# Window attention of a vision block: the row maxima in seven groups of 8 by 8 queries instead of eight of 8 by 7

## The chip, the cores and the metric

The kernel runs on one core of a Trainium2 chip. Its time is the device time of one execution, in microseconds (us). Below, PE is TensorE (PEld its weight loads), DVE is VectorE, ACT is ScalarE, POOL is GpSimd and SP is SyncE, which here only issues DMAs. ACTq and SPq are the DMA issues of ACT and SP.

## The reference

Two images of 128 channels and 56 by 56 pixels go through three attentions that are mixed by a gate, a gated MLP and a LayerNorm. The change touches only the third attention: every pixel looks at the 7 by 7 pixels around it (edge padded), in 8 heads of 16 channels.

```python
DIM, HEADS, BS, TOPK, WIN = (128, 8, 8, 4, 7)
padded = jnp.pad(feat, ((0, 0), (pad, pad), (pad, pad), (0, 0)), mode='edge')
patches = jnp.stack([padded[:, dy:dy + Hx, dx:dx + Wx, :] for dy in range(WIN) for dx in range(WIN)], axis=3)
...
q = _lin(Q, wq_w[2], wq_b[2]).reshape(Bx, Nq, h, d)
k = _lin(patches, wk_w[2], wk_b[2]).reshape(Bx, Nq, WIN * WIN, h, d)
v = _lin(patches, wv_w[2], wv_b[2]).reshape(Bx, Nq, WIN * WIN, h, d)
attn = jax.nn.softmax(jnp.einsum('bnhd,bnwhd->bnhw', q, k) * scale, axis=-1)
y_win = jnp.einsum('bnhw,bnwhd->bnhd', attn, v).reshape(Bx, Nq, C)
```

## The kernel before

The program has three stages: projections with the two block attentions (to about 331 us), the window attention (to about 560 us), and the MLP. Only the window attention changes.

**Jobs and steps.** The window attention has 14 jobs: two images by seven bands of 8 pixel rows. A band is 56 columns by 8 rows, 448 queries, and its keys are 62 columns by 14 rows. A job is 14 steps: the keys come in 7 blocks of 9 columns, each done for 4 heads at a time. All engines run one loop over steps `q` (`STEP_RANGE`), and the place in a job is `r = q % 14`. In every step PE does the scores of step q (L881: 4 matmuls, keys by queries, 120, 72 or 64 queries wide), ACT the exponential of them (L1083), and PE the products with the values for step q - 3 (L897). Scores alternate between two PSUM banks, so scores of step q wait for the exponential of step q - 2.

**The maxima.** Softmax needs a number to subtract from each query's scores before the exponential. It rides in the score matmul: row 126 and 127 of `Q` hold minus the maximum as two bf16 parts. It is made 12 steps (`LEAD`) before the job's first step. One group of maxima, here called A0 to A7, is `maxima` on PE (L840): 8 matmuls, one a head, of 64 queries by 182 keys, into a slot of two PSUM banks. A subgroup is 7 columns of 8 rows, 56 queries; the matmul takes 64 columns of queries and the last 8 repeat. DVE reduces a slot over the keys (L1456). Every two groups DVE splits the result into two bf16 parts (L1462, L1464), PE transposes it (L867, here called S0 to S3), DVE copies the transpose to `nT` (L1469), and SP sends `nT` by DMA into rows 126 and 127 of `Q` (L450). Scores of the steps in `TILE_NEEDED` wait for that DMA.

**Slots.** Groups A, transposes S, and two jobs at a band's end share two slots in turn: D (L908, `spread` times `RB`, the reciprocal sums brought to all channels; DVE multiplies by them, L1474) and Y (L914, the output projection; DVE adds it to `XT`, L1484). Use n of the slots waits until DVE has read use n - 2 (`slot_free`). Where each stands is a list of steps:

```python
MAX_AT = (0, 1, 3, 5, 7, 8, 10, 12)
BEHIND = 1
TURN_AT = (4, 8, 11, 15)
TILE_NEEDED = {0: 0, 2: 1, 6: 2, 8: 3}
SUMS_AT, RECIP_AT, PARTS_AT, NORM_AT, Y_AT = 17, 21, 22, 27, 30
```

With the lead of 12, `MAX_AT` 0 stands at r = 2, and so on: before, A0 to A7 stand at r = 2, 3, 5, 7, 9, 10, 12, 0 and S0 to S3 at r = 6, 10, 13, 3. The group `BEHIND` is done after the step's products, not ahead of its scores. D stands at r = 13 behind the products, Y at r = 2 behind the products.

**The chain to D.** At r = 3 SP moves the sums of the job that just ended to `SR` (L464). At r = 7 DVE takes the reciprocal (L1446), ahead of everything else that it has in that step. POOL multiplies by the gate and splits into three bf16 parts (L587 to L597, which counts `w_parts`). At r = 8 SP sends them to `RB` in three DMAs (L471). D waits for them.

**SP's list.** SP issues DMAs in the order of its program and waits where a wait stands. For step q it takes in turn: the `nT` transfer of a transpose that stands in step q - 1 (it waits for DVE's copy), a load of values `Vw` in even steps (L459), the sums, and the three transfers to `RB`. ACT issues the loads of a later band's keys and queries (L384, L386) in its own stream, behind the exponentials of r = 13, 3 and 7; the largest part goes at r = 13.

Of the kernel before, what the change touches and what calls it, by code (L numbers as in the profile page):

```python
# [36 lines left out]
KCOLS = SUBC + WIN - 1  # L37
# [7 lines left out]
MQ = 64  # L45
# [7 lines left out]
QSPAN = HEADS * BAND + MQ - SUB  # L53
# [72 lines left out]
def build(nc, x, wts, vecs, rows, pjb, dwr, c32, cmask, out):  # L126
    ctx = ExitStack()
    with ctx:
# [108 lines left out]
        with ExitStack() as s3:  # L237
            K = [KQ0[:, 0:KSPAN]] + [sb(f"K{n}", [128, KSPAN], BF16, s3)[:] for n in (1, 2)]
            QB = [KQ0[:, KSPAN:KSPAN + QSPAN]] + [sb(f"Q{n}", [128, QSPAN], BF16, s3)[:] for n in (1, 2)]
            Q = [q[:, 0:HEADS * BAND].rearrange("p (h n) -> p h n", h=HEADS) for q in QB]  # L240
            Vw = [sb(f"Vw{n}", [KEYS, VROW], F32, s3) for n in range(VRING)]
            P = [sb(f"P{n}", [KEYS, 4 * max(BQ)], F32, s3) for n in range(4)]
            wn = [sb(f"wn{n}", [128, 2, PAIRS], F32, s3) for n in range(2)]
            wnb = [sb(f"wnb{n}", [128, 2, 2, PAIRS], BF16, s3) for n in range(2)]
            nT = [sb(f"nT{n}", [HEADS, 2, TILE], BF16, s3) for n in range(2)]
# [76 lines left out]
        SUBN = SUBS * JOBS  # L322
# [5 lines left out]
        MAX_AT = (0, 1, 3, 5, 7, 8, 10, 12)  # L328
        BEHIND = 1
        TURN_AT = (4, 8, 11, 15)  # L330
        TILE_NEEDED = {0: 0, 2: 1, 6: 2, 8: 3}
# [10 lines left out]
        def turned_at(q):  # L342
            found = []
            for k, at0 in enumerate(TURN_AT):
                j = job_at(q + LEAD, at0)
                if j is not None:
                    found.append(TILES * j + k)
            return found

        pa, pa_order = {}, {}  # L350
        for q in STEP_RANGE:
            jobs, behind = [], []
            for k, at0 in enumerate(MAX_AT):
                if job_at(q + LEAD, at0) is not None:
                    (behind if k == BEHIND else jobs).append(("A", SUBS * job_at(q + LEAD, at0) + k))
# [10 lines left out]
        assert sum(k == "A" for k, n in pa_order) == SUBN  # L366
# [22 lines left out]
        def _(sp):  # L389
# [51 lines left out]
            for q in STEP_RANGE:  # L441
# [4 lines left out]
                for n in turned_at(q - 1):  # L446
                    j, c = divmod(n, TILES)
# [38 lines left out]
        def _(pool):  # L486
# [132 lines left out]
        def _(pe):  # L619
# [204 lines left out]
            pe.wait_ge(sem("w_pad"), 2 * BUFS)  # L824
# [7 lines left out]
            def maxima(n, slot, order):  # L832
                j, c = divmod(n, SUBS)
# [3 lines left out]
                for h in range(HEADS):  # L837
                    p, e = divmod(h, 2)
                    first = h * KBAND + SUBC * c * KROWS
                    last = mm(PS[MQ * e:MQ * (e + 1), 2 * slot + p // 2, p % 2 * SKEYS:(p % 2 + 1) * SKEYS],  # L840
                              QB[j % BUFS][0:SHIFT0, h * BAND + c * SUB:h * BAND + c * SUB + MQ], K[j % BUFS][0:SHIFT0, first:first + SKEYS], start=True, stop=True)
# [12 lines left out]
            for q in STEP_RANGE:  # L854
# [4 lines left out]
                for kind, n, slot, order in pa.get(q, ()):  # L859
                    if kind == "A" and n % SUBS != BEHIND:  # L860
                        maxima(n, slot, order)
                    if kind == "S":
# [3 lines left out]
                        for c in range(2):  # L866
# [309 lines left out]
        def _(dve):  # L1176
# [261 lines left out]
            for q in STEP_RANGE:  # L1438
# [9 lines left out]
                for kind, n, slot, order in pa.get(q, ()):  # L1448
                    dve.wait_ge(sem("w_slot"), order + 1)
                    if kind == "A":  # L1450
                        tl, c = divmod(n, 2)
# [5 lines left out]
                        if c == 1:  # L1457
# [7 lines left out]
                    if kind == "S":  # L1465
                        if n >= 2:
                            dve.wait_ge(sem(f"w_shift{n % 2}"), 16 * (n // 2))
                        src = PS[0:HEADS, 2 * slot, 0:128].bitcast(BF16).rearrange("p (s e n) -> p e s n", s=2, e=2)[:, :, :, 0:SUB]
                        ve.tensor_copy(nT[n % 2][:].rearrange("p e (s n) -> p e s n", s=2), src).then_inc(sem("w_slot_read"), 1)  # L1469
# [144 lines left out]
```

## Time and profile before

| what | value |
|---|---|
| median of 3 runs | 770.14 us (766.46 to 771.43) |
| the profiled execution, its own time | 772.19 us |
| span of its trace | 770.4 us |
| busy: PE, DVE, ACT, POOL | 689.2, 607.4, 351.2, 214.8 us |
| mean granted TensorE clock | 0.962 |

The span is what the trace covers, and the profiled execution's own time is 1.8 us more. Busy time says how long an engine had an instruction in it, not what it waited for. The 14139 instructions of the trace are read below by stretches of the window attention, since what a change in one stage is worth is decided there.

### The profile page before, as it was taken

How to read it: one execution, taken by the hardware profiler on the slowest of the kernel's cores; microseconds unless marked ns; L12 is line 12 of the kernel's file. 1: busy time of each engine (PE TensorE's matmuls, PEld its weight loads, DVE VectorE, ACT ScalarE, POOL GpSimd, SP SyncE). 2: the span in 40 equal slices, each digit the busy share in tenths (PEclk: the TensorE clock that was granted, in tenths of full speed). 3: DMA queues.
4: the chain of work that ended last, by engine and by line, in shares of the span. 5: the costliest groups of instructions: out<-in, count | busy, mean ns of one | idle time of the engine just before them, and what ended most of it. 6: DMA issues, size and time to landing. Idle time of an engine off the chain costs nothing.

```text
span 770.4 us, 14139 instructions
## 1 busy us (share of the span) xinstructions
PE 689.2 (89%) x5055; PEld 365.3 (47%) x5055; DVE 607.4 (79%) x1236; ACT 351.2 (46%) x618; POOL 214.8 (28%) x331
## 2 busy tenths in 40 slices
PE   4998987789788989878999999999889999999996
PEld 2543443445344444444555555555434545455553
DVE  6996657878788799867777777777369879999873
ACT  2175423444444344305555555555534062646676
POOL 2026112545445454507100110010190436400000
PEclk9999988979999899969999999999999999999998
DMA  6004221533233339724656656762000000000101
GB/s 245 0 0 109 54 54 45 132 80 79 71 81 93 81 95 252 176 72 131 158 154 180 180 156 167 181 171 47 18 2 0 1 0 0 1 21 22 42 22 63
DMA packets 52663, 66.22 MB, mean 86 GB/s; under 512 B 10606, under 2 KB 48498, under 8 KB 50738
## 3 DMA queue, kind: packets, MB, share of 16 engines
q1 hardware_dynamic: 49426, 43.08, 21.3%
q10 hardware_dynamic: 3168, 22.24, 10.5%
q8 instruction: 41, 0.67, 0.4%
q14 instruction: 28, 0.23, 0.1%
HBM read 43.03 MB, written 21.57 MB: 84 GB/s over the span
## 4 chain that ended last, share of the span: by engine, by line
PE 50%; DVE 22%; issue 8%; ACT 6%; DMA 2%; POOL 1%; SPq 0%; ACTq 0%; DVEq 0%; POOLq 0%
PE banks L959 12%; PE banks L897 7%; PE banks L881 6%; PE banks L840 5%; DVE AC L1204 4%; DVE mx L1392 4%; PE banks L914 3%; DVE sm L1407 2%; DVE X L1484 2%; PE banks L852 2%; DVE SEB L1395 1%; PE banks L710 1%; ACT pf L1022 1%; ACT PTB L1067 1%; PE banks L782 1%
## 5 line engine op out<-in xcount | busy, mean ns | idle before, releaser
L1083 ACT ACTIVATE P<-banks 126x480 f32<-126x480 f32 (+2 forms) x196 | 101.1, 521 | 112.1 <-PE banks L881 98.6
L959 PE MATMUL banks<-FP,PTB 128*128 128x392 f32 x384 | 129.8, 493 | 2.1 <-DVE c L1487 1.2
L1456 DVE TENSOR_REDUCE wn<-banks 128x4 f32<-128x728 f32 x112 | 102.1, 913 | 26.0 <-PE banks L840 24.2
L1204 DVE SCALAR_TENSOR_TENSOR AC<-XT,vec,AC 128x1540 f32<-128x1540 f32 (+5 forms) x48 | 118.0, 2462 | 1.1
L959 PEld LDWEIGHTS banks<-FP,PTB 128*128 128x128 f32 x384 | 72.7, 190 | 56.9 <-DVE FP L1524 2.2
L549 POOL TENSOR_TENSOR SEB<-SEB,rg 112x392 f32<-112x392 f32 x112 | 61.2, 567 | 111.2 <-DVE rg L1414 111.2
L1058 ACT ACTIVATE SEB<-SEB 112x424 f32<-112x424 f32 x56 | 31.2, 558 | 113.1 <-DVE SEB L1395 113.1
L897 PE MATMUL banks<-P,Vw 126*17 126x120 f32 (+2 forms) x1568 | 73.3, 260 | 0.0
L519 POOL TENSOR_TENSOR pk<-pr,pk 128x434 bf16<-128x434 f32 (+1 forms) x42 | 47.7, 1136 | 45.4 <-DVE pk L1307 45.4
L804 PE MATMUL banks<-PTB,VP 106*128 106x448 f32 x112 | 54.0, 570 | 6.2 <-issue 3.7
L782 PE MATMUL banks<-Af,XT 128*112 128x424 f32 x112 | 54.2, 568 | 0.0
L587 POOL TENSOR_TENSOR SR<-SR,SRG 64x56 f32<-64x56 f32 x14 | 4.2, 297 | 171.6 <-DVE SR L1446 171.6
L1302 DVE TENSOR_TENSOR pr<-pf,pk 128x434 f32<-128x434 f32 (+1 forms) x42 | 27.6, 658 | 27.1 <-ACT pk L1023 27.0
L881 PE MATMUL banks<-Q,K 128*128 128x120 bf16 (+2 forms) x504 | 45.2, 213 | 2.0 <-DMA Q<-nT 1.7
L1392 DVE TENSOR_REDUCE mx<-banks 112x8 f32<-112x392 f32 x112 | 36.8, 370 | 10.3 <-PE banks L783 10.3
L840 PE MATMUL banks<-K,Q 126*64 126x182 bf16 x576 | 37.0, 251 | 3.3 <-DVE c L1486 3.0
L1395 DVE TENSOR_TENSOR SEB<-banks,mx 112x392 f32<-112x392 f32 x112 | 37.2, 374 | 1.9
L791 PE MATMUL banks<-cst,SEB 112*106 112x112 f32 x224 | 34.5, 278 | 4.3 <-POOL SEB L549 4.2
L1204 DVE SCALAR_TENSOR_TENSOR FP<-X,vec,FP 128x3025 f32<-128x3025 f32 (+5 forms) x16 | 36.2, 2263 | 0.6
L643 PE MATMUL banks<-X,diag 128*128 128x440 f32 (+3 forms) x90 | 35.0, 552 | 1.3 <-DMA X<-in_x 1.3
L1407 DVE TENSOR_REDUCE sm<-SEB 112x8 f32<-112x392 f32 x112 | 36.1, 364 | 0.0
L881 PEld LDWEIGHTS banks<-Q,K 128*128 128x128 bf16 x504 | 26.1, 98 | 20.7 <-issue 6.0
(247 smaller groups left out, 1195.6 us busy)
## 6 DMA issues: line engine op xcount, KB each, us to landing
k_parts<-pk SPq DMA_DIRECT2D x84, 108.5 KB, 3.4
Vw<-v_rows SPq DMA_DIRECT2D x84, 66.9 KB
q_parts<-pk SPq DMA_DIRECT2D x42, 112.0 KB, 2.3
K<-k_parts ACTq DMA_DIRECT2D x7, 651.0 KB, 5.8
v_rows<-vst SPq DMA_DIRECT2D x14, 263.5 KB
X<-in_x SPq DMA_DIRECT2D x2, 1568.0 KB, 8.3
K<-k_parts ACTq DMA_DIRECT2D x7, 434.0 KB, 3.7
out_y<-zs SPq DMA_DIRECT2D x7, 392.0 KB, 2.4
```

Of the source, the lines that this page charges most:

```text
L549: g.tensor_tensor(dst, src, by, ALU.mult).then_inc(sem("c_norm"), 1)
L782: mm(s, XT[:, img, ds(t * BAND + c * TILE, TILE)], Af[img][:], start=True, stop=False)
L804: last = mm(bank(4 + img, C, BAND), VP[img][:, j, :], PT[img][:, j, :], start=(j == 0), stop=(j == PAIRS - 1))
L840: last = mm(PS[MQ * e:MQ * (e + 1), 2 * slot + p // 2, p % 2 * SKEYS:(p % 2 + 1) * SKEYS], QB[j % BUFS][0:SHIFT0, h * BAND + c * SUB:h * B ...
L881: last = mm(PS[:, 4 + q % 2, g * BQ[b]:(g + 1) * BQ[b]], K[j % BUFS][:, first:first + 128], Q[j % BUFS][:, h, BLOCK * BX0[b]:BLOCK * BX0[b ...
L897: last = mm(PS[QUAD * g:QUAD * g + VH, 6 + u, BLOCK * BX0[b]:BLOCK * BX0[b] + BQ[b]], Vw[s % VRING][0:BKEYS[b], VH * h:VH * (h + 1)], P[p ...
L959: last = mm(bank(2 + place_in_unit, C, ZPIX), WT[:, dy, part, C * grp:C * (grp + 1)], D[:, part, QROWS * q + dy:QROWS * (q + 1) + dy, :].r ...
L1083: a(P[q % 4][0:BKEYS[b], 0:4 * BQ[b]], PS[0:BKEYS[b], 4 + q % 2, 0:4 * BQ[b]], ACT.Exp).then_inc(sem("w_exp"), 1)
L1204: return ve.scalar_tensor_tensor(out=o, in0=src(ro + dy, rn, co + dx, cn), scalar=v(wcol + t), in1=o, op0=ALU.mult, op1=ALU.add)
L1392: ve.tensor_reduce(mx[:, ty, :, :], groups(ps, ty), AX.X, ALU.max).then_inc(sem("c_max"), 1)
L1407: ve.tensor_reduce(sm[:, ty, :, :], groups(Ex[r % 2], ty), AX.X, ALU.add).then_inc(sem("c_sum"), 1)
L1456: ve.tensor_reduce(dst, src, AX.X, ALU.max, negate=True).then_inc(sem("w_slot_read"), 1)
```

## The change

A group of maxima takes 8 by 8 queries, 64 of 64 useful, and 14 by 14 = 196 keys instead of 13 by 14 = 182. A job then has seven groups, A0 to A6. Tiles of two groups are 128 queries wide instead of 112, and the fourth tile of a job holds one group: one transpose, and a `nT` transfer half as wide. The padding of `Q` and its three memsets go. The places in the steps change with it: A0 to A6 stand at r = 2, 4, 6, 7, 9, 10, 0 and S0 to S3 at r = 7, 10, 13, 3. The fourth tile is needed at r = 10 instead of 8. Everything else keeps its place.

```diff
-KCOLS = SUBC + WIN - 1
+MCOLS = 8
+MGROUPS = SIDE // MCOLS
+MTILES = -(-MGROUPS // 2)
+KCOLS = MCOLS + WIN - 1
...
-MQ = 64
+MQ = BLOCK * MCOLS
...
-        MAX_AT = (0, 1, 3, 5, 7, 8, 10, 12)
+        MAX_AT = (0, 2, 4, 5, 7, 8, 12)
         BEHIND = 1
-        TURN_AT = (4, 8, 11, 15)
-        TILE_NEEDED = {0: 0, 2: 1, 6: 2, 8: 3}
+        TURN_AT = (5, 8, 11, 15)
+        TILE_NEEDED = {0: 0, 2: 1, 6: 2, 10: 3}
...
+        def tile_groups(k):
+            return min(2, MGROUPS - 2 * k)
...
-                    dst = Q[j % BUFS][SHIFT0:SHIFT0 + 2, :, c * TILE:(c + 1) * TILE]
-                    sp.dma_start(dst, nT[n % 2][:]).then_inc(sem(f"w_shift{n % 2}"), 16)
+                    cols = tile_groups(c) * MQ
+                    dst = Q[j % BUFS][SHIFT0:SHIFT0 + 2, :, 2 * MQ * c:2 * MQ * c + cols]
+                    sp.dma_start(dst, nT[n % 2][:, :, 0:cols]).then_inc(sem(f"w_shift{n % 2}"), 16)
...
-                        for c in range(2):
+                        for c in range(tile_groups(n % MTILES)):
...
-                        if c == 1:
+                        if c == tile_groups(k // 2) - 1:
```

On PE, from the step r = 4 of a job (before: from the end of r = 3) to r = 7, with A groups as L840 before and L846 now, the transpose as L867 and L873, scores L881 and L887, products L897 and L903. Before:

```order
L840 MATMUL banks<-FP 64x182 x8
L881 MATMUL banks<-Q,K 128x120 x4
L897 MATMUL banks<-P,Vw 17x72 x4
L840 MATMUL banks<-FP 64x182 x8
L881 MATMUL banks<-Q,K 128x120 x4
L897 MATMUL banks<-P,Vw 17x120 x4
L867 MATMUL banks<-identb,wnb 8x128 x2
L881 MATMUL banks<-Q,K 128x120 x4
L897 MATMUL banks<-P,Vw 17x120 x4
L840 MATMUL banks<-FP 64x182 x8
```

Now:

```order
L887 MATMUL banks<-Q,K 128x120 x4
L903 MATMUL banks<-P,Vw 17x72 x4
L846 MATMUL banks<-FP 64x196 x8
L887 MATMUL banks<-Q,K 128x120 x4
L903 MATMUL banks<-P,Vw 17x120 x4
L846 MATMUL banks<-FP 64x196 x8
L887 MATMUL banks<-Q,K 128x120 x4
L903 MATMUL banks<-P,Vw 17x120 x4
L846 MATMUL banks<-FP 64x196 x8
L873 MATMUL banks<-identb,wnb 8x128 x2
```

A1 has moved behind the products of r = 4, A2 to the head of r = 6, and the transpose S0, which stood alone at the head of r = 6, now stands in r = 7 right behind A3.

On DVE, in the same place of the program, from the reduction of A1 on (reductions L1456 and L1463, split L1462/L1464 and L1469/L1471, copy to `nT` L1469 and L1477, reciprocal L1446 and L1452). Before:

```order
L1456 TENSOR_REDUCE wn0<-banks 128x4 [waits w_slot]
L1462 CAST wnb0<-wn0 128x2x4 [waits w_slot,w_slot_read]
L1464 TENSOR_TENSOR wnb0<-wn0,wnb0 128x2x4 [waits w_high]
L1456 TENSOR_REDUCE wn1<-banks 128x4 [waits w_split,w_slot]
L1469 COPY nT0<-banks 8x224 [waits w_shift0,w_slot]
L1446 RECIPROCAL SR0<-SR0 64x56 [waits w_recips0,w_sums0]
L1456 TENSOR_REDUCE wn1<-banks 128x4 [waits w_slot]
L1462 CAST wnb1<-wn1 128x2x4 [waits w_slot,w_slot_read]
L1464 TENSOR_TENSOR wnb1<-wn1,wnb1 128x2x4 [waits w_high]
```

Now:

```order
L1463 TENSOR_REDUCE wn0<-banks 128x4 [waits w_slot]
L1469 CAST wnb0<-wn0 128x2x4 [waits w_slot,w_slot_read]
L1471 TENSOR_TENSOR wnb0<-wn0,wnb0 128x2x4 [waits w_high]
L1463 TENSOR_REDUCE wn1<-banks 128x4 [waits w_split,w_slot]
L1452 RECIPROCAL SR0<-SR0 64x56 [waits w_recips0,w_sums0]
L1463 TENSOR_REDUCE wn1<-banks 128x4 [waits w_slot]
L1469 CAST wnb1<-wn1 128x2x4 [waits w_slot,w_slot_read]
L1471 TENSOR_TENSOR wnb1<-wn1,wnb1 128x2x4 [waits w_high]
L1477 COPY nT0<-banks 8x256 [waits w_shift0,w_slot]
```

The copy of S0 to `nT0` stood ahead of the reciprocal and now stands behind it and behind the reduction and the split of A3.

On SP, from r = 7 to r = 11 (`nT` transfers L450 and L457, values L459 and L466, `RB` L471 and L478). Before:

```order
L450 DMA Q1<-nT0 2x8x112 [waits w_slot_read]
L459 DMA Vw6<-v_rows 126x1x136 [waits w_products]
L471 DMA RB0<-SB0 4x16x56 [waits rb_zero,w_parts]
L471 DMA RB0<-SB0 4x16x56 x2
L459 DMA Vw7<-v_rows 126x1x136 [waits w_products]
L450 DMA Q1<-nT1 2x8x112 [waits w_slot_read]
```

Now:

```order
L457 DMA Q1<-nT0 2x8x128 [waits w_slot_read]
L466 DMA Vw6<-v_rows 126x1x136 [waits w_products]
L478 DMA RB0<-SB0 4x16x56 [waits rb_zero,w_parts]
L478 DMA RB0<-SB0 4x16x56 x2
L466 DMA Vw7<-v_rows 126x1x136 [waits w_products]
L457 DMA Q1<-nT1 2x8x128 [waits w_slot_read]
```

Only the width of the `nT` rows differs: the transfer of S0 stands ahead of the three to `RB` and the transfer of S1 behind them, before and now.

## Rows read from the trace of the kernel before

**Rows 1.** Stretch 405 to 420 us: busy time by engine, granted clock, DMA share, GB/s
```profile
405.00:420.00 15.00, 14.54 (x246) 8.29 (x238) 11.66 (x25) 8.00 (x16) 1.41 (x6) 1.00 0.62 168
```

**Rows 2.** PE's timeline in one job: start, us, line, op, [idle before <- releaser]
```profile
443.32 0.51 PE L840 MATMUL banks<-K,Q 126*64 126x182 bf16 x8
443.76 0.38 PE L881 MATMUL banks<-FP 128*128 128x120 bf16 x4
...
444.40 0.51 PE L840 MATMUL banks<-K,Q 126*64 126x182 bf16 x8
...
445.13 0.38 PE L881 MATMUL banks<-FP 128*128 128x120 bf16 x4
...
448.06 0.55 PE L908 MATMUL banks<-RB,spread 128*128 128x448 bf16 x2
...
450.45 0.38 PE L881 MATMUL banks<-Q,K 128*128 128x120 bf16 x4
...
453.98 0.50 PE L840 MATMUL banks<-K,Q 126*64 126x182 bf16 x8 [0.44 <-DVE c L1486]
...
454.98 0.50 PE L840 MATMUL banks<-K,Q 126*64 126x182 bf16 x8
```

**Rows 3.** DVE's timeline in the same job
```profile
441.38 0.25 DVE L1469 COPY nT<-banks 8x224 bf16<-8x224 bf16 x1
441.56 0.48 DVE L1446 RECIPROCAL SR<-SR 64x56 f32<-64x56 f32 x1
...
444.95 0.92 DVE L1456 TENSOR_REDUCE wn<-banks 128x4 f32<-128x728 f32 x1 [0.16 <-PE banks L840]
...
446.19 0.26 DVE L1469 COPY nT<-banks 8x224 bf16<-8x224 bf16 x1
...
454.53 0.92 DVE L1456 TENSOR_REDUCE wn<-banks 128x4 f32<-128x728 f32 x1 [0.34 <-PE banks L840]
...
455.77 0.91 DVE L1456 TENSOR_REDUCE wn<-banks 128x4 f32<-128x728 f32 x1
...
456.78 0.48 DVE L1446 RECIPROCAL SR<-SR 64x56 f32<-64x56 f32 x1
```

**Rows 4.** SP's own DMA issues in the same job
```profile
441.66 0.71 SPq L450 DMA_DIRECT2D Q<-nT  x1
442.42 0.78 SPq L459 DMA_DIRECT2D Vw<-v_rows  x1
443.91 2.37 SPq L471 DMA_DIRECT2D RB<-SB  x3
446.32 0.83 SPq L459 DMA_DIRECT2D Vw<-v_rows  x1
447.20 0.70 SPq L450 DMA_DIRECT2D Q<-nT  x1
```

**Rows 5.** ACT's issue of a band's largest load, same job
```profile
447.84 0.56 ACTq L384 DMA_DIRECT2D FP<-k_parts  x1
```

**Rows 6.** DVE groups by shape, 100 to 330 us
```profile
L1392 DVE TENSOR_REDUCE mx<-banks 112x8 f32<-112x392 f32 x56 | 31.4, 560 | 10.3 <-PE banks L783 10.3
```

**Rows 7.** DMA issues from 376 to 528 us: KB each, median us to landing
```profile
K<-k_parts ACTq DMA_DIRECT2D x6, 651.0 KB, 5.8
...
Q<-q_parts ACTq DMA_DIRECT2D x6, 336.0 KB, 6.7
```

**Rows 8.** The second job: S3's transfer issued, and the scores that wait for it
```profile
361.14 0.69 SPq L450 DMA_DIRECT2D Q<-nT  x1
...
366.32 0.38 PE L881 MATMUL banks<-Q,K 128*128 128x120 bf16 x4 [1.42 <-DMA Q<-nT]
```

**Rows 9.** The stage's end: the transfers to RB and the D behind them
```profile
547.66 1.84 SPq L471 DMA_DIRECT2D RB<-SB  x3
...
550.96 0.55 PE L908 MATMUL banks<-RB,spread 128*128 128x448 bf16 x2
```

**Rows 10.** The stage's start: the last group ahead of the first scores
```profile
341.50 0.82 PE L840 MATMUL banks<-FP 126*64 126x182 bf16 x8 [0.70 <-DVE wn L1456]
```

More of the change, by code:

```diff
@@ L52 @@
 KSPAN = HEADS * KBAND + 64
-QSPAN = HEADS * BAND + MQ - SUB
+QSPAN = HEADS * BAND
 QUAD = 32
@@ L244, in build @@
             wnb = [sb(f"wnb{n}", [128, 2, 2, PAIRS], BF16, s3) for n in range(2)]
-            nT = [sb(f"nT{n}", [HEADS, 2, TILE], BF16, s3) for n in range(2)]
+            nT = [sb(f"nT{n}", [HEADS, 2, 2 * MQ], BF16, s3) for n in range(2)]
             OB = [sb(f"OB{n}", [128, 2, BAND], F32, s3) for n in range(2)]
@@ L321, in build @@
         STEPS = STEPJ * JOBS
-        SUBN = SUBS * JOBS
+        GROUPS_ALL = MGROUPS * JOBS
         LEAD = 12
@@ L346, in turned_at @@
                 if j is not None:
[L347 removed]
+                    found.append(MTILES * j + k)
             return found
@@ L354, in build @@
                 if job_at(q + LEAD, at0) is not None:
-                    (behind if k == BEHIND else jobs).append(("A", SUBS * job_at(q + LEAD, at0) + k))
+                    (behind if k == BEHIND else jobs).append(("A", MGROUPS * job_at(q + LEAD, at0) + k))
             jobs += [("S", n) for n in turned_at(q)]
@@ L365, in build @@
                 pa.setdefault(q, []).append((kind, n, order % 2, order))
-        assert sum(k == "A" for k, n in pa_order) == SUBN
+        assert sum(k == "A" for k, n in pa_order) == GROUPS_ALL
+        def tile_groups(k):
+            return min(2, MGROUPS - 2 * k)
         NQ = IMAGES * QUARTERS
@@ L832, in maxima @@
             def maxima(n, slot, order):
-                j, c = divmod(n, SUBS)
+                j, c = divmod(n, MGROUPS)
                 if c == 0:
@@ L838, in maxima @@
                     p, e = divmod(h, 2)
-                    first = h * KBAND + SUBC * c * KROWS
+                    first = h * KBAND + MCOLS * c * KROWS
                     last = mm(PS[MQ * e:MQ * (e + 1), 2 * slot + p // 2, p % 2 * SKEYS:(p % 2 + 1) * SKEYS],
-                              QB[j % BUFS][0:SHIFT0, h * BAND + c * SUB:h * BAND + c * SUB + MQ], K[j % BUFS][0:SHIFT0, first:first + SKEYS], start=True, stop=True)
+                              QB[j % BUFS][0:SHIFT0, h * BAND + c * MQ:h * BAND + (c + 1) * MQ], K[j % BUFS][0:SHIFT0, first:first + SKEYS], start=True, stop=True)
                 last.then_inc(sem("w_slot"), 1)
@@ L859, in _ @@
                 for kind, n, slot, order in pa.get(q, ()):
-                    if kind == "A" and n % SUBS != BEHIND:
+                    if kind == "A" and n % MGROUPS != BEHIND:
                         maxima(n, slot, order)
@@ L901, in _ @@
                 for kind, n, slot, order in pa.get(q, ()):
-                    if kind == "A" and n % SUBS == BEHIND:
+                    if kind == "A" and n % MGROUPS == BEHIND:
                         maxima(n, slot, order)
@@ L1450, in _ @@
                     if kind == "A":
-                        tl, c = divmod(n, 2)
+                        j, k = divmod(n, MGROUPS)
+                        tl, c = MTILES * j + k // 2, k % 2
                         if c == 0 and tl >= 2:
@@ L1467, in _ @@
                             dve.wait_ge(sem(f"w_shift{n % 2}"), 16 * (n // 2))
-                        src = PS[0:HEADS, 2 * slot, 0:128].bitcast(BF16).rearrange("p (s e n) -> p e s n", s=2, e=2)[:, :, :, 0:SUB]
-                        ve.tensor_copy(nT[n % 2][:].rearrange("p e (s n) -> p e s n", s=2), src).then_inc(sem("w_slot_read"), 1)
+                        parts = tile_groups(n % MTILES)
+                        src = PS[0:HEADS, 2 * slot, 0:MQ * parts].bitcast(BF16).rearrange("p (s e n) -> p e s n", s=parts, e=2)
+                        ve.tensor_copy(nT[n % 2][:, :, 0:MQ * parts].rearrange("p e (s n) -> p e s n", s=parts), src).then_inc(sem("w_slot_read"), 1)
                     if kind == "D":
```

7 lines of the change are left out of this document (3 added, 4 removed).

## The prediction

> **What bounds the kernel now.** I read the stretches of the window attention first. In the full pace of that stage PE is busy 14.54 of 15.00 us at full granted clock and DVE 11.66 [rows 1]. So PE's own row of work sets the pace, and DVE has room of a fifth. Then I read PE's timeline over one job: a group of maxima holds PE for 0.44 us (443.32 to 443.76), and scores and products of a step for 0.64 us (443.76 to 444.40) [rows 2]. The one wait of any size in a job is 0.44 us ahead of A1, for DVE's reading of Y. A job takes 15.22 us, from one reciprocal to the next (441.56 to 456.78) [rows 3]. Last I read what is nearly late, because a planned order moves work against deadlines that no busy share shows: D waits for three DMAs that start with the reciprocal, and each tile's maxima must have landed in `Q` before its scores. I measure all from R, the start of the reciprocal. Before, SP issues the transfer of S0 at R + 0.10, the values, then RB at R + 2.35, S1's transfer at R + 5.64 [rows 4]; ACT issues the largest band load at R + 6.28 [rows 5]; D runs at R + 6.50 [rows 2].
>
> **Sizes of the pieces now.** A group is 14 keys wider of 182, so at most 0.44 x 14/182 = 0.034 us longer: 0.47. A reduction of 392 elements takes 0.560 us and one of 728 takes 0.92 [rows 3, 6], 1.07 ns an element, so 784 elements take 0.98. DVE does seven of 0.98 instead of eight of 0.92, 0.5 us less a job; it is not the bound, so that alone is worth nothing. The lone transpose of the fourth tile saves about 0.1: a pair with its short wait fills 445.13 - 444.40 - 0.44 = 0.29 [rows 2]. The padding memsets are on POOL ahead of the stage and worth 0.
>
> **PE's row of work, D to the next R.** Before, D to A1 is 453.98 - 448.06 = 5.92 [rows 2]. Now two groups in it are wider (+0.06), S3 is half (-0.10), the wait for Y goes (-0.44), since A1 stands one step later, and that step's scores and products come ahead of A1 (454.98 - 453.98 - 0.44 = 0.56). That makes 6.00, and A1 ends at 6.47. But A2 now stands only one step before the reciprocal, so DVE decides R: 0.11 from A1's end to its reduction, 1.24 + 0.06 to A2's (454.53 to 455.77), 0.89 for A2's reduction until the next instruction starts (1.01 to the reciprocal less 0.18 for the copy between, + 0.06) [rows 2, 3]. R comes at 6.47 + 0.11 + 1.30 + 0.89 = 8.77 after D; before it was 8.72.
>
> **PE's row of work, R to D.** Before 6.50. A3 now lies ahead of R (-0.44), r = 12 has no group (-0.44), A4 and A5 are wider (+0.06). S0 shares a slot with A2, so it waits until A2 is reduced, at R + 0.09, and about 0.1 for the release, and takes 0.2 (+0.40). PE is ready for it 0.64 + 0.47 + 0.64 + 0.47 = 2.22 after A1's end, DVE at 2.5: a new wait of 0.3. S1, with a longer reduction ahead, +0.06. D could run at R + 6.14. By PE alone a job would be 8.77 + 6.14 = 14.91, a gain of 0.3. This is what the change could bring.
>
> **The first cost: SP's list.** SP's order is the same before and now, and there lies the trouble. S0's transfer stands ahead of RB and waits for DVE's copy. Before, the copy ended at R + 0.07. Now it is behind the reciprocal (0.42, with the 0.06 to 0.08 that neighbouring DVE instructions overlap), and from a reduction that closes a tile to the end of its copy it is 446.19 + 0.26 - 444.95 = 1.50, + 0.06 [rows 3]: R + 1.98. Then 0.76 for S0's issue and 0.82 for the values [rows 4]: RB starts at R + 3.58 instead of R + 2.35, though POOL has the parts ready as early as before. Three issues take 1.84 [rows 9] to 2.37 [rows 4]; I take 2.2: R + 5.78. Landing is bounded from above by the stage's end, where D ran 1.46 after the last issue's end (550.96 - 549.50) [rows 9], from below by 0. I take 1.4, since a DMA of any kind here needs more than 3 us from its issue to its landing [rows 7]. D runs at R + 7.25, so a job takes 16.0: +0.8. With the lower end D is not late at all, and with the upper it is +1.0.
>
> **The second cost: what stands behind RB.** The values and then S1's transfer follow at R + 5.82 and R + 6.70. ACT's largest load does not wait for D; it goes 0.22 before D's place in PE's row (448.06 - 447.84) [rows 2, 5]: R + 5.92. Before, S1's transfer went 0.64 ahead of this load; now it goes 0.8 behind it. What that costs the trace shows once: S3's transfer in the second job, issued at 361.14 among band loads, held its scores until 366.32, 5.2 us [rows 8]. The load itself needs 5.8 us, and its queries, issued 0.6 later, 6.7 [rows 7]. So S1's maxima land between R + 11.7 and R + 13.2; I take the middle, 12.5. If the transfer slipped through as before, where it was there within 450.45 - 447.20 = 3.25 [rows 2, 4], it would land by R + 9.95. The scores of r = 2 need it 450.45 - 448.06 + 0.06 = 2.45 after D, at R + 9.7. They wait 2.8 us, and R follows 8.77 - 2.45 = 6.32 later. A job takes 12.5 + 6.32 = 18.8 us, +3.6 (from +2.8 to +4.3). While that wait is last, D's exact time costs nothing.
>
> The Trainium skill ("DMA: Bandwidth & Descriptors", section "Queues, rings and completion order") says that each DMA engine takes turns between the rings of SP and ACT, a packet at a time. By that rule a small transfer need not wait for a whole band load; the 5.2 us speak against it here. By the rule the time would be that of the first rival.
>
> **The sum.** There are 14 jobs. S0, RB and S1 of three neighbouring jobs meet in 12 job times, and in 10 of them the largest load goes too (it stops three bands before the end). 10 x 3.6 + 2 x 0.8 = 37.6. Gains: ahead of the first scores there is one group less, 0.82 + 0.70 = 1.5 [rows 10]; the wait of 1.42 [rows 8] goes, since the fourth tile is needed two steps later, and the first job has PE's gain of 0.3: together 3. So +34.6 on the profiled execution's 772.2, 806.8. The median shown is 2.05 lower: **804.8 us**, 4.5% slower.
>
> **Rivals.** (1) S1's transfer passes the band load, and only D is late: 12 x 0.8 - 3 = +6.6, **777 us**. For it: transfers issued just ahead of a load pass. Against: the 5.2 us. (2) RB's last transfer is caught too: it is issued about 0.7 ahead of the load, as S1's was before, and that one passed; this margin is thin. Then D runs at R + 5.92 + 5.8 + 0.1 = 11.8, a job takes 20.6 (+5.4, up to +6.9): 54 + 1.6 - 3 = +52.6, **823 us**, up to 838. (3) The other side: SP does not hold RB back, as S0's copy is done early enough. RB, S0 and S1 then run as before and PE's gain stays: 13 x 0.3 + 3 = -7, **763 us**, faster. It decides at a copy that ends by R + 0.75 (RB at R + 2.35); I have 1.98, and DVE's order puts 1.5 us of work between, so it needs the copy to be there at less than half of that. (4) The stage's PE falls to a lower granted clock in the new waits. Rows of before have full clock at 14.54 busy of 15; with waits of 4 us in 19 nothing here shows a fall, and I price it only in the upper end.
>
> **Chances.** My forecast 60%, (1) 15%, (2) 12%, (3) 9%, the rest 4%. The range takes in (1) at its lower part and most of (2): 775 to 830. A measurement of this kernel tells 1%, about 7.7 us, from no change. Faster by more than that needs (3) to do better than I price it: 5%. Within it lie most of (3) and half of (1): 14%. Slower: 81%.
>
> **What would show it.** In the profile of the changed kernel: the reduction at 0.98 us; reciprocals 18.8 us apart (16.0 in the last two jobs); RB's issues 3.6 us behind the reciprocal; a wait of about 1.1 us of D for the DMA to RB and one of about 2.8 of the scores at r = 2 for the DMA from `nT`; no wait of A1 for Y. I am wrong if S1's transfer is issued ahead of the large load, if the `nT` wait is under 1 us, or if S0's copy comes within 1 us of the reciprocal.

## The result and the profile after

The changed kernel takes 816.31 us (median of 4 runs, 815.39 to 820.88), the kernel before 769.21 beside it (4 runs, 766.46 to 771.43). The ratio is 1.063, with a 95% interval from 1.057 to 1.068: slower, by more than the 4.5% forecast and inside the range. The profiled execution took 815.39 us, its span is 813.2, the mean granted clock 0.950.

The whole page says little. PE was busy 689.2 us and is now busy 697.1. These are the page's busy times, and two of its groups with the waits ahead of them, and the chain that ended last by line:

```profile
PE 697.1 (86%) x4929; PEld 364.7 (45%) x4929; DVE 602.2 (74%) x1222; ACT 349.4 (43%) x618; POOL 215.7 (27%) x328
...
PE banks L965 13%; DMA Q<-nT 5%; PE banks L887 5%; PE banks L903 4%; PE banks L920 4%; DVE mx L1398 4%; DVE wn L1463 3%; DMA FP<-nT 3%; PE banks L846 2%; DVE AC L1210 2%; DVE sm L1413 2%; PE banks L858 1%; DVE SEB L1401 1%; ACT pf L1028 1%; ACT PTB L1073 1%
...
L1463 DVE TENSOR_REDUCE wn<-banks 128x4 f32<-128x784 f32 x98 | 94.2, 965 | 21.7 <-PE banks L846 20.2
...
L887 PE MATMUL banks<-Q,K 128*128 128x120 bf16 (+2 forms) x504 | 47.3, 220 | 18.7 <-DMA Q<-nT 17.9
```

The reduction takes 0.965 us (0.98 forecast). Two transfers from `nT`, into `Q` and into `FP` (the same kind of buffer, the bands use both in turn), hold 8% of the chain. PE's waits in the window attention say how often (us in total, times, longest):

```profile
PE banks L887 <- DMA Q<-nT: 17.9, 7, 3.4
PE banks L914 <- DMA RB<-SB: 10.1, 12, 1.3
PE banks L887 <- DMA FP<-nT: 6.8, 3, 3.0
```

Scores wait for the maxima of S1 in ten jobs, 24.7 us in all. D waits in twelve jobs, 10.1 in all. Both counts are those of the forecast. The kernel before had 1.7 us of waits for `nT` in two waits, and none of D.

**One job, from its reciprocal at R = 461.04.** First DVE's timeline (start, us, line, operation): the copy of S0 comes behind the reciprocal and A3's reduction, as in the order.

```profile
461.04 0.48 DVE L1452 RECIPROCAL SR<-SR 64x56 f32<-64x56 f32 x1
461.44 0.90 DVE L1463 TENSOR_REDUCE wn<-banks 128x4 f32<-128x784 f32 x1
...
462.69 0.27 DVE L1477 COPY nT<-banks 8x256 bf16<-8x256 bf16 x1
```

Then SP's own issues, and ACT's of the largest load. They answer to [rows 4, 5]:

```profile
462.99 0.71 SPq L457 DMA_DIRECT2D Q<-nT  x1
463.75 0.78 SPq L466 DMA_DIRECT2D Vw<-v_rows  x1
464.62 1.93 SPq L478 DMA_DIRECT2D RB<-SB  x3
466.60 0.83 SPq L466 DMA_DIRECT2D Vw<-v_rows  x1
467.48 0.70 SPq L457 DMA_DIRECT2D Q<-nT  x1
```

```profile
466.93 0.56 ACTq L390 DMA_DIRECT2D FP<-k_parts  x1
```

RB is issued at R + 3.58 (2.35 before). S1's transfer goes at R + 6.44 and the load at R + 5.89: the transfer was 0.64 ahead of the load and is now 0.55 behind it. PE's timeline shows the two waits, and the projection Y (L920) behind the second:

```profile
467.98 0.55 PE L914 MATMUL banks<-RB,spread 128*128 128x448 bf16 x2 [0.76 <-DMA RB<-SB]
...
473.11 0.58 PE L887 MATMUL banks<-Q,K 128*128 128x120 bf16 x4 [2.63 <-DMA Q<-nT]
...
473.97 3.36 PE L920 MATMUL banks<-ON,W 128*128 128x448 f32 x4
```

D runs at R + 6.94, the scores at R + 12.07. The next reciprocal comes at 481.78, so this job takes 20.74 us. Y takes 3.36, and it takes 1.77 in the kernel before. The same four matmuls of scores take 0.58, and 0.38 before [rows 2].

**What S1's transfer waits for.** The trace also holds a record of every DMA packet. ACT's load is 48 packets of 13,888 bytes. In this job they start between 468.65 and 470.93, and the last has ended by 471.86. S1's transfer is 16 packets of 256 bytes, of about 0.03 us each. They start at 471.70 to 471.98, which is 4.2 us behind the issue at 467.48 and 1.1 us ahead of the scores. From 468.86 to 471.69 only ACT's queue (q10; SP's is q1) has packets: those of the load, and the first of the queries' load behind it (packets, MB, share of 16 engines):

```profile
q10 hardware_dynamic: 63, 0.59, 77.7%
```

In the kernel before, S1's transfer was issued at 447.20. Its 16 packets (224 bytes) start at 448.56 to 448.68, and the first of the load at 449.19. So the transfer itself is short in both. Behind the load it doesn't start before nearly all of the load has been moved.

**All jobs.** Windows cut from one reciprocal to the next, four of the ten with an S1 wait (length, busy of PE, PEld, DVE, ACT, POOL, then the granted clock, DMA share, GB/s):

```profile
424.18:442.23 18.05, 14.66 (x237) 8.18 (x237) 11.37 (x27) 7.94 (x16) 1.43 (x6) 1.00 0.53 144
442.23:461.04 18.81, 16.07 (x237) 8.59 (x237) 11.35 (x27) 8.05 (x16) 1.43 (x6) 0.91 0.51 140
461.04:481.78 20.74, 17.05 (x237) 9.05 (x237) 11.34 (x26) 8.02 (x16) 1.43 (x6) 0.84 0.47 124
481.78:499.89 18.11, 13.85 (x221) 7.75 (x221) 11.38 (x27) 7.33 (x15) 1.43 (x6) 1.00 0.53 134
```

Only two of the ten have the full clock. They take 18.05 and 18.11 us; the other eight take 18.81 to 20.84 with clocks of 0.84 to 0.92. The ten take 196.34 us (363.47 to 559.81) where the kernel before took 152.63 (365.06 to 517.69): +43.7. The last jobs add 0.8. The stage begins with the first group of maxima. These are its lines, first before, then now:

```profile
332.14 0.89 PE L840 MATMUL banks<-FP 126*64 126x182 bf16 x16 [1.92 <-DVE banks L1435]
327.73 0.87 PE L846 MATMUL banks<-FP 126*64 126x196 bf16 x16 [1.92 <-DVE banks L1441]
```

From there to the first reciprocal it takes 32.92 us before and 35.75 now: +2.8. From the first group to the last reciprocal that is 223.46 and 270.78 us: +47.3, as much as the medians differ (47.1). So the window attention holds all of the difference. The two spans differ by only 813.2 - 770.4 = 42.8, because in this execution the stages ahead, which the change leaves as they are but for three memsets, ended 4.4 us earlier. In the fourteen traces of this record the first group starts anywhere from 324.72 to 332.14. In the two jobs of full clock S1's maxima are the limit and nothing else is late. In the rest a second cost comes on top, which I had given no chance of its own: a lower clock.

### The profile page after: what moved, and what is told of

The parts are those of the page before. It is cut to its first block, busy times and chain, and to the rows that moved or that the text cites. A ratio compares the mean times of both kernels' runs of the same rounds, so it can differ in the third digit from the quotient of the medians.

```text
span 813.2 us, 13870 instructions
## 1 busy us (share of the span) xinstructions
PE 697.1 (86%) x4929; PEld 364.7 (45%) x4929; DVE 602.2 (74%) x1222; ACT 349.4 (43%) x618; POOL 215.7 (27%) x328
## 4 chain that ended last, share of the span: by engine, by line
PE 42%; DVE 22%; DMA 9%; issue 8%; ACT 6%; SPq 1%; POOL 1%; ACTq 1%; DVEq 0%; POOLq 0%
PE banks L965 13%; DMA Q<-nT 5%; PE banks L887 5%; PE banks L903 4%; PE banks L920 4%; DVE mx L1398 4%; DVE wn L1463 3%; DMA FP<-nT 3%; PE banks L846 2%; DVE AC L1210 2%; DVE sm L1413 2%; PE banks L858 1%; DVE SEB L1401 1%; ACT pf L1028 1%; ACT PTB L1073 1%
## 5 line engine op out<-in xcount | busy, mean ns | idle before, releaser
L1463 DVE TENSOR_REDUCE wn<-banks 128x4 f32<-128x784 f32 x98 | 94.2, 965 | 21.7 <-PE banks L846 20.2
L903 PE MATMUL banks<-P,Vw 126*17 126x120 f32 (+2 forms) x1568 | 75.0, 266 | 0.0
L887 PE MATMUL banks<-Q,K 128*128 128x120 bf16 (+2 forms) x504 | 47.3, 220 | 18.7 <-DMA Q<-nT 17.9
L788 PE MATMUL banks<-Af,XT 128*112 128x424 f32 x112 | 52.1, 548 | 0.0
L1492 DVE TENSOR_TENSOR X<-banks,XT 128x448 f32<-128x448 f32 x14 | 14.0, 999 | 48.3 <-PE banks L920 48.3
L887 PEld LDWEIGHTS banks<-Q,K 128*128 128x128 bf16 x504 | 27.4, 101 | 39.1 <-DMA Q<-nT 19.4
L1482 DVE TENSOR_TENSOR ON<-OB,banks 128x896 f32<-128x896 f32 x14 | 15.2, 1087 | 33.3 <-PE banks L914 33.3
```

The source lines that it names most:

```text
L788: mm(s, XT[:, img, ds(t * BAND + c * TILE, TILE)], Af[img][:], start=True, stop=False)
L887: last = mm(PS[:, 4 + q % 2, g * BQ[b]:(g + 1) * BQ[b]], K[j % BUFS][:, first:first + 128], Q[j % BUFS][:, h, BLOCK * BX0[b]:BLOCK * BX0[b ...
L903: last = mm(PS[QUAD * g:QUAD * g + VH, 6 + u, BLOCK * BX0[b]:BLOCK * BX0[b] + BQ[b]], Vw[s % VRING][0:BKEYS[b], VH * h:VH * (h + 1)], P[p ...
L1463: ve.tensor_reduce(dst, src, AX.X, ALU.max, negate=True).then_inc(sem("w_slot_read"), 1)
```

## The experiments

**1. The groups without the places.** The new geometry, with A0 to A6 and S0 to S3 in the steps that they had before. From the changed kernel:

```diff
-        MAX_AT = (0, 2, 4, 5, 7, 8, 12)
+        MAX_AT = (0, 1, 3, 5, 7, 8, 12)
-        TURN_AT = (5, 8, 11, 15)
+        TURN_AT = (4, 8, 11, 15)
```

> Seven groups of 8 by 8 at the places of before (MAX_AT 0, 1, 3, 5, 7, 8, 12 and TURN_AT 4, 8, 11, 15), so that S0 is copied ahead of the reciprocal again. My theory (the time is lost to two late transfers, which come from the place of S0): about 763 us, 760 to 767, RB issued 2.35 us behind the reciprocal, no wait of the scores for nT over 1 us. Rival (the wider groups themselves, with reductions of 0.97 us, cost the time by waits of PE for DVE): over 790 us.

Measured: 773.43 us (9 runs) beside 768.6, ratio 1.004 (0.9999 to 1.008). The loss is gone, but 760 to 767 was expected, and the gain isn't there; experiments 11 and 12 show why. Nearly all jobs are 14.99 us apart (before 15.22), but one takes 21.25. In it SP's three issues to `RB` took 2.85 us instead of 2.2:

```profile
472.21 2.85 SPq L478 DMA_DIRECT2D RB<-SB  x3
...
475.98 0.71 SPq L457 DMA_DIRECT2D FP<-nT  x1
```

```profile
482.76 0.58 PE L887 MATMUL banks<-FP 128*128 128x120 bf16 x4 [3.78 <-DMA FP<-nT]
...
483.62 3.36 PE L920 MATMUL banks<-ON,W 128*128 128x448 f32 x4
```

In a usual job S1's transfer goes 0.40 us ahead of the load (445.35 and 445.75); here 0.65 us more of SP's time put it 0.16 behind, and 6 us were lost. The faster jobs have used up part of a margin that was 0.64 to 1.12 us in the ten jobs of the kernel before.

**2. The places without the groups.** The kernel before, with eight groups of 8 by 7, in the new steps:

```diff
-        MAX_AT = (0, 1, 3, 5, 7, 8, 10, 12)
+        MAX_AT = (0, 2, 4, 5, 7, 8, 10, 12)
-        TURN_AT = (4, 8, 11, 15)
+        TURN_AT = (5, 8, 11, 15)
```

> The kernel before, eight groups of 8 by 7, with only the places moved: A1, A2 and S0 one step later, the rest as before. My theory: most of the loss is here too, 790 to 820 us. S1's transfer is then issued only 0.1 to 0.4 us behind the largest load, since A6 still stands at r = 12, so some jobs may escape the long wait. Rival (wider groups cost): 770 us, no change.

Measured: 817.56 us (4 runs), ratio 1.064 (1.058 to 1.071), the time of the changed kernel. PE's waits are the same ones:

```profile
PE banks L881 <- DMA Q<-nT: 18.0, 7, 3.3
PE banks L881 <- DMA FP<-nT: 7.5, 3, 2.7
PE banks L908 <- DMA RB<-SB: 4.9, 12, 0.5
```

So the places alone make the whole loss. D mostly runs at about R + 6.95 in both. It waits half as long here (4.9 against 10.1) because PE comes to it later, and the time is the same. S1's transfer is issued 0.11 to 0.20 us behind the load in all ten jobs, and all ten wait; none escapes.

**3. The largest load one step later.** The changed kernel, with S1's transfer ahead of the load again and D still late:

```diff
-                for part, off in enumerate((0, 4, 8)):
+                for part, off in enumerate((1, 4, 8)):
```

> The changed kernel with the largest band load one step later in ACT's stream (r = 0 of the next job instead of r = 13), so that it is issued more than 1 us behind S1's transfer. My theory: the waits of about 2.6 us of the scores at r = 2 go, D stays 0.8 us late, 767 to 776 us. Rival (the wait comes from SP's late issue alone, whatever ACT loads): no gain, about 815 us.

Measured: 785.52 us (4 runs), ratio 1.021 (1.014 to 1.027). The wait for `nT` falls from 24.7 us to 1.8 and D's stays (11.6 in 12). Moving one load takes back two thirds of the loss, so the collision of this load with this transfer is the main cause. I missed by some 10 us. The jobs are 16.2 apart, as forecast for a late D alone, but only in part for that reason: D at R + 6.98 is 0.5 later than in the kernel before. The rest goes with a new wait. The reciprocal waits for the sums' DMA, which now stands behind the moved load, 5.4 us in seven waits (0.5 in one before this edit):

```profile
DVE SR L1452 <- DMA SR<-OB: 5.4, 7, 1.8
```

The first reciprocal came at 368.47 instead of 363.47, but the stage itself began 3.4 of these 5.0 us later.

**4. RB ahead of S0's transfer in SP's list.** The changed kernel, with SP's block for `RB` moved ahead of the `nT` transfers of its step, so that D is in time:

```diff
+                j = job_at(q, PARTS_AT)
+                if j is not None:
+                    sp.wait_ge(sem("w_parts"), j + 1)
...
                 for n in turned_at(q - 1):
```

> The changed kernel with the three RB transfers ahead of S0's transfer in SP's list, nothing else. My theory: D is no longer late, but S1's transfer is still issued about 1 us behind the largest load, and that wait is the last, so the time hardly falls: 808 to 820 us. Rival (D's lateness is what costs): D's wait of 10.1 us in all comes back, 800 to 806 us or less.

Measured: 836.44 us (4 runs), ratio 1.089 (1.081 to 1.096). Worse than the change itself, and above both ranges. D no longer waits, but S0's transfer stands behind RB, and S1's behind both: at R = 432.00 S1's is issued at 439.00 with the load at 437.89, so it is 1.1 us behind the load and not 0.55. The scores wait until R + 13.2:

```profile
438.11 0.55 PE L914 MATMUL banks<-RB,spread 128*128 128x448 bf16 x2
...
445.18 0.58 PE L887 MATMUL banks<-Q,K 128*128 128x120 bf16 x4 [4.39 <-DMA Q<-nT]
...
446.04 3.35 PE L920 MATMUL banks<-ON,W 128*128 128x448 f32 x4
```

The ten jobs take 21.50 us on average (366.86 to 581.84). In this job the packets of S1's transfer start at 444.13, behind those of the load and also behind those of the queries' load, of which the last starts at 443.81. D runs 0.8 us earlier than in the changed kernel, and no job is shorter for it. Mending the first lateness lengthens the second, and the second sets the loop.

**5. Both.** RB first, and the load one step later, the edits of experiments 3 and 4 together:

> The changed kernel with both edits together: RB ahead of S0's transfer on SP, and the largest band load one step later on ACT. My theory: both waits go, jobs of 15.0 to 15.5 us, 765 to 775 us. Rival (the places themselves cost, by S0 behind A3 and the reciprocal behind two reductions): 780 us or more.

Measured: 776.89 us (4 runs), ratio 1.010 (1.001 to 1.019). Most jobs take 15.25 to 16.2 us, and the wait for `nT` is 6.3 us in 19 small ones of at most 0.9. With both waits undone the changed kernel comes within 1% of the one before. That is 2 us above my range and below the rival's. What is left of the loss stands beside two more waits: DVE's copies to `nT` wait 17.9 us in 12 for the transfers out of it, which now go behind RB, and the reciprocal 4.1 us in 8 for the sums. What the places cost without these was not separated.

**6. The old places and the later load.** Experiment 1 with the edit of experiment 3:

> The new groups at the old places, with the largest band load one step later, so that S1's transfer has over 1 us of lead on it instead of 0.4. My theory: the occasional long job of the new groups at the old places (21.2 us once in its trace, against 15.0) goes, and the time is 761 to 768 us. Rival (the long job has another cause, or the load now delays the sums): 770 us or more.

Measured: 770.39 us (10 runs), ratio 1.002 (0.999 to 1.005). Jobs are mostly 15.0 apart, none is long, and the time is still that of the kernel before. So the long job was this collision, but the time lies in the rival's range: the gain isn't there.

**7. S1's transfer late, in the kernel before.** This was to move the transfer behind the load with nothing else changed:

```diff
-        TURN_AT = (4, 8, 11, 15)
+        TURN_AT = (4, 10, 11, 15)
```

> The kernel before with only the transpose S1 two steps later (TURN_AT 4, 10, 11, 15), so that its transfer is issued behind the largest band load while RB and D keep their times. My theory (a small transfer issued behind the load waits for it): waits of 3 to 4 us of the scores at r = 2 in 10 or 11 jobs, 805 to 825 us. Rival (the collision needs SP's delayed list): 768 to 775 us.

Measured: 778.29 us (10 runs), ratio 1.013 (1.010 to 1.016). It wasn't the test that I meant. PE waited 0.35 us a job at the transpose for DVE (`wn`), so ACT's load came later too: in one job the transfer was issued at 449.28 and the load at 449.77, and in all ten it was still 0.25 to 0.49 ahead. No S1 wait came; the one `nT` wait, of 2.1 us, is at another tile. So it doesn't test the collision; it shows only that a lead of 0.25 us is enough. Experiment 9 is the test.

**8. Work for PE in the wait.** The changed kernel with 30 extra matmuls ahead of the wait for S1's maxima, in the ten jobs. Their result is overwritten and used by nothing; they only keep PE busy.

```diff
+                    if q >= 2:
+                        pe.wait_ge(sem("w_exp"), q - 1)
+                    if r == 2 and 2 <= j <= 11:
+                        for _ in range(30):
+                            mm(PS[:, 4 + q % 2, 0:128], identb[:], identb[:], start=True, stop=True)
                     if r in TILE_NEEDED:
                         n = MTILES * j + TILE_NEEDED[r]
                         pe.wait_ge(sem(f"w_shift{n % 2}"), (n // 2 + 1) * 16)
-                    if q >= 2:
-                        pe.wait_ge(sem("w_exp"), q - 1)
```

> The changed kernel with 30 extra matmuls of 128 columns (about 2.4 us of work that nothing uses, overwritten by the next scores) in jobs 2 to 11, placed where PE waits for S1's maxima at r = 2. If a part of the loss is the granted clock that falls in this wait and makes the work behind it slow (Y took 3.36 us instead of 1.77), the clock stays at 1.00 and the time falls to 803 to 810 us although PE does more. Rival (the clock is no part of it): 816 us or more.

Measured: 802.9 us (4 runs), ratio 1.043 (1.035 to 1.052). That is 13.4 us less than the changed kernel, with more work on PE (1.85 us of it a job) and the same late transfers. PE's timeline at the same place:

```profile
443.34 1.85 PE L883 MATMUL banks<-identb 128*128 128x128 bf16 x30
...
445.86 1.77 PE L923 MATMUL banks<-ON,W 128*128 128x448 f32 x4
```

and the window of 20 us there:

```profile
440.00:460.00 20.00, 17.99 (x294) 10.59 (x289) 12.21 (x26) 8.29 (x18) 1.44 (x6) 1.00 0.52 143
```

Y is back at 1.77, the clock at 1.00, and jobs take 17.8 to 18.9 us, most of them like the two full-clock jobs of the changed kernel. D's wait is unchanged (9.9 us in 12).

**9. S1's transfer behind the load, in the kernel before.** SP issues it behind the values of the next even step; all else is as before, D in time too:

```diff
                 for n in turned_at(q - 1):
-                    j, c = divmod(n, TILES)
...
+                    if n % TILES != 1:
+                        maxima_rows(n)
...
+                for n in turned_at(q - 2):
+                    if n % TILES == 1:
+                        maxima_rows(n)
```

> The kernel before with one edit in SP's list: S1's transfer of the maxima is issued behind the values of r = 12 instead of ahead of them, about 0.2 us behind the largest band load instead of 0.6 us ahead of it. PE's, DVE's and ACT's order, RB and D are untouched. My theory (a small transfer that is issued behind the load waits for it): the scores at r = 2 wait 3 to 4 us in most of jobs 1 to 11, the clock falls in it, 800 to 835 us. Rival (by the page's rule the engines take turns and it passes; then it is 0.8 us later and still in time): 766 to 773 us.

Measured: 806.94 us (4 runs) beside 770.47, ratio 1.049 (1.039 to 1.060). SP's issues, ACT's, and PE's timeline in one job:

```profile
449.73 2.35 SPq L479 DMA_DIRECT2D RB<-SB  x3
452.12 1.68 SPq L463 DMA_DIRECT2D Vw<-v_rows  x2
453.85 1.45 SPq L450 DMA_DIRECT2D Q<-nT  x2
```

```profile
453.67 0.56 ACTq L384 DMA_DIRECT2D FP<-k_parts  x1
```

```profile
453.89 0.55 PE L916 MATMUL banks<-RB,spread 128*128 128x448 bf16 x2
459.03 0.38 PE L889 MATMUL banks<-Q,K 128*128 128x120 bf16 x4 [2.68 <-DMA Q<-nT]
459.58 2.90 PE L922 MATMUL banks<-ON,W 128*128 128x448 f32 x4
```

The transfer is issued 0.18 us behind the load and is waited for until 5.36 us after the load's issue. Seven jobs have such a wait, 23.9 us in all. The other three of the ten pass, with 15.2 to 16.1 us a job. The issue times tell them apart, since SP's time for the issues varies from job to job: in the seven the transfer goes between 0.18 us behind the load and 0.06 ahead of it, in the three 0.23, 0.27 and 1.01 ahead. The other traces agree: every S1 transfer with a lead of 0.25 us or more was there in time or nearly (waits of at most 0.23 us, in experiment 5), and every one issued behind the load was waited for, but for one job of experiment 8, where the added work filled the wait. This is the collision alone, old groups and old places, and it costs 4.9%.

**10. The new places, mended another way.** The changed kernel with the later load and, instead of SP's new order, the reciprocal and the parts one step earlier:

```diff
-        SUMS_AT, RECIP_AT, PARTS_AT, NORM_AT, Y_AT = 17, 21, 22, 27, 30
+        SUMS_AT, RECIP_AT, PARTS_AT, NORM_AT, Y_AT = 17, 20, 21, 27, 30
```

> The changed kernel (new groups, new places) with the reciprocal and the RB transfers one step earlier (RECIP_AT 20, PARTS_AT 21), so that RB is issued ahead of S0's transfer and D is in time, and the largest band load one step later. My theory (nothing is wrong with the groups or with A1 behind Y; only the two deadlines were missed): jobs of 14.8 to 15.3 us, 758 to 770 us, no slower than before. Rival (the new places cost by themselves): over 776 us. A risk in it: the sums must have landed one step earlier, and the later load stands ahead of them.

Measured: 793.79 us (4 runs), ratio 1.034 (1.027 to 1.040). I missed by more than 20 us. The risk that I had named is what came. The reciprocal is now ahead of its input: the sums are issued behind the moved load, and DVE, which works in order, holds A2's reduction behind the reciprocal, and PE's transpose behind that. The waits say so:

```profile
DVE SR L1452 <- DMA SR<-OB: 13.0, 10, 2.7
...
PE banks L873 <- DVE wn L1463: 20.0, 13, 3.4
```

**11 and 12. A wider margin for S1's transfer.** SP issues the values of r = 10 behind S1's transfer instead of ahead of it, once on experiment 1 and once, as its control, on the kernel before:

```diff
-                s = q // 2 + AHEAD
-                if q % 2 == 0 and 0 <= s < BLOCKS * JOBS:
+                due = q - 1 if q % STEPJ == 11 else q
+                s = due // 2 + AHEAD
+                if q % STEPJ != 10 and due % 2 == 0 and 0 <= s < BLOCKS * JOBS:
```

> The new groups at the old places, and on SP the values of r = 10 behind S1's transfer instead of ahead of it, so that this transfer is issued about 0.9 us ahead of the largest load (0.4 before), with ACT's loads where they were. My theory (the gain of the groups is 0.2 us a job and about 3 us at the stage's start, and what ate it was a margin that was too thin): no long job, 761 to 767 us, 0.5 to 1 per cent faster than the kernel before. Rival (the groups gain nothing): 769 us or more.

> The kernel before with the same edit on SP alone, as a control for the last: S1's transfer ahead of the values of r = 10. It had 0.6 us of lead and no long job in its trace, so 766 to 771 us, no change. If it is faster by 1 per cent, the kernel before had long jobs too, and the gain of the last run is not the groups'.

Measured: 769.4 us (12 runs) beside 770.55, ratio 1.001 (0.998 to 1.004), and 773.14 (12 runs), ratio 1.003 (1.000 to 1.006). Both lie above what was expected, the first in its rival's range. With the new groups jobs are 15.0 us apart and none is long: from the first reciprocal to the last it takes 186.9 us, 190.6 in the control and in the kernel before. But the start of the stage gives it back. From the first group of maxima to the first reciprocal it takes 37.6 us here, 34.8 in experiment 6 and 34.2 in experiment 1, against 32.9 before and 32.7 in the control, so the whole stage takes 224.6 us against 223.5 before. At the start POOL has a block of work of its own (L575 to L585 in the changed kernel, 343.54 to 357.13), and while it runs some of DVE's short splits take 1.7 us instead of 0.17: two in the kernel before, three with the new groups. PE waits for one of them, here in the changed kernel:

```profile
353.55 0.38 PE L873 MATMUL banks<-identb,wnb 128*8 128x128 bf16 x2 [2.24 <-DVE wnb L1471]
```

That these splits are the cause was not tested apart; the first jobs also wait for `nT` and for the sums (1.8 and 1.9 us in experiment 11). Beside its control, which has the same list on SP, experiment 11 is the faster one: its mean is 2.4 us lower, with a 95% interval of about 0.3 to 4.6 from the twelve runs of each. Beside the kernel before it is not, and the control itself came out 0.3% above the kernel before with a stage just as long (223.3 us). So seven groups instead of eight are worth 0.2 us a job, the start takes most or all of it back, and what is left over is well under 1%.

## Why the prediction was right, and what of it was off

**Sizes of the pieces.** Right. The reduction takes 0.965 us for 0.98 forecast, and DVE's half a microsecond a job didn't show in the time of the changed kernel.

**The first cost, SP's list.** Right: RB is issued at R + 3.58 to 3.61 in nine of the twelve jobs, as forecast, though the terms of the forecast add up to 3.56 and the copy ended 0.06 earlier than said. The three issues took 1.93 us, not 2.2, so all behind them was 0.3 earlier: D mostly at R + 6.94 to 7.03, not 7.25, and its wait is 10.1 / 12 = 0.84 us, not 1.1. The forecast's own terms, 5.78 + 1.4, give 7.18. The 1.4 was taken "since a DMA of any kind here needs more than 3 us"; the rows shown for it are two large loads, and D runs 1.97 us after the start of the last RB issue, so that reason is wrong. The last two jobs lost 0.15 and 0.64 instead of 0.8 each. The second is D's lateness (0.60). In the first D is 0.5 later, but the kernel before had an unusually long way from D to the reciprocal there, 9.08 us instead of 8.72. That D's exact time costs nothing while S1 is late fits experiment 4, where D runs 0.8 earlier and the jobs are longer.

**The second cost, what stands behind RB.** The mechanism is shown three times: experiment 3 moves the load away and takes back 31 us, experiment 9 moves only the transfer and loses 36, and experiment 4 moves the transfer further behind and loses 20 more. The size was a little too large. I took the middle between R + 11.7 and R + 13.2. The scores of the ten jobs ran between R + 11.1 and R + 13.1, on average at R + 12.07. From S1's issue to the scores it is 4.6 to 6.5 us here, 5.5 on average, and 5.2 to 6.9 in experiment 9, so the 5.2 us of [rows 8] were a fair guide, on the low side. In the two full-clock jobs the scores' run to the next reciprocal is 6.29 and 6.30 us where I had 6.32. At full clock, with the average landing, the term would have been 10 x (12.07 + 6.30 - 15.22) = 31.5, not 36.

The page "DMA: Bandwidth & Descriptors" of the Trainium skill (section "Queues, rings and completion order") has each DMA engine take turns between rings, but drain a whole packet of one ring, typically 9 to 17 descriptors, ahead of a turn. The prediction concluded from it that a small transfer need not wait for a whole load. The packet records don't bear that conclusion out: S1's pieces of 256 bytes start when nearly all 48 pieces of the load have been moved. That isn't against the page. If the 48 pieces are spread evenly over the 16 engines, each has three, which by the page's figure (an estimate) fit into one turn. No run here changed the number of pieces, so whether this is the reason stays open.

**The step that failed, in size only: "a job takes 12.5 + 6.32".** The 6.32 stood for work at the clock of the kernel before. In the job above it took 8.67 (473.11 to 481.78), Y 3.36 in place of 1.77. I had written of rival (4) that "nothing here shows a fall, and I price it only in the upper end". The ten jobs average 19.63, with 7.56 from the scores to the next reciprocal instead of 6.32; experiment 8 gave 13.4 back by keeping PE busy, and there that part was 6.29 again. My term was 4 us too large by the landing and 12 too small by the clock. In a sum of +34.6 where +47 was measured these two errors are of opposite sign, so the closeness of the total is partly luck.

**The start, a second failed term.** 3 us of gain were forecast, and the stage's start takes 2.8 us more: an error of 6 us. Ahead of the first scores 1.1 us are gained (forecast 1.5: from the first group to the scores 10.11 us before, 9.05 now), and behind them 3.9 are lost. The sum had no term for DVE's long splits and the waits behind them. The wait of 1.42 [rows 8], counted as a gain in full, was worth 0.15: the job that holds it took 15.37 us beside 15.22.

**The rivals.** (1), the transfer passes the load: refuted by the ten waits, and by experiment 9. (2), RB is caught too: it isn't. Its last transfer is issued 0.92 us ahead of the load in the job above and passes; D ran at R + 7.11 at the latest in ten of the twelve jobs, and at 7.50 and 7.64 where RB itself went 0.5 and 0.65 later. (3), SP doesn't hold RB back: refuted, the copy ended at 462.96, R + 1.92. And PE's own gain, "by PE alone a job would be 14.91", was never seen with the new places: with the large load in them the best jobs of experiment 5 take 15.25, and one without it 15.04. What it rests on stays untested.

**What stays open.** Why a transfer behind the load isn't started earlier, and why the start is longer with the new groups, as said above. And why the clock falls behind some waits and not behind others. In the changed kernel Y took 2.38 to 3.36 us behind eight waits of 1.61 to 3.41 us, and 1.77 behind two of 2.31 and 2.33. Length alone doesn't sort them. Behind the waits of experiment 8, of at most 1.20 us, it never fell.

## What to carry to other kernels

When a planned order moves a copy or a transpose, follow it past the compute engines into the in-order list that issues DMAs: everything behind it there moves too, and what it moves can cross a large load that another engine issues at its own time. Write down each such lead before the change (here 0.64 us at the least); what it guards is a cliff, not a slope: here the transfer passed with a lead of 0.23 us, and with one of 0.06 the scores waited 4.3 us for it. When two things become late, mend the one that is last, and expect a worse time from mending only the first; and price a new wait of PE with the clock that follows it, not with its length alone. When two traces are compared, measure the changed stage from its own first instruction, since what runs ahead of it can end several microseconds earlier or later by chance.

## What the runs showed of the hardware that I had not expected

A wait of PE costs more than its length. Behind a wait of 2.63 us the same four matmuls took 3.36 us where they take 1.77, a ratio of 1.90, which is near that of the two clock levels, 2.4 and 1.2 GHz. The window of that job has a granted clock of 0.84. Thirty matmuls that compute nothing, put into the wait, made the kernel 13 us faster.

A transfer of 16 packets of 224 bytes issued 0.18 us behind a load of 651 KB is there for the scores only 5.2 us later, and one issued 0.23 us ahead of the load costs no wait. With a lead of 0.06 us it was still caught, with a wait of 4.26 us. All three are jobs of experiment 9. The packets themselves take 0.03 us each; they start when nearly all of the load has been moved.

DVE's short splits (128 x 8, 0.17 us) take 1.7 us two or three times at the stage's start, while POOL is at its block of work.

SP's time for the same three issues is not fixed: 1.84 [rows 9], 1.93, 2.09, 2.35, 2.37 [rows 4] and 2.85 us in these runs. In experiment 1 that spread alone moved a transfer across the load and cost 6 us of one job.
